# Perceiver block on one core: loop order of the cross-attention, keys and values between the scores and the turns of the probabilities

## The reference, cut to what matters

```
q = (layernorm(x) @ wq.T + bq)          # 16 heads of 8
k = (ctx @ wk.T + bk);  v = (ctx @ wv.T + bv)
scores = einsum('bhqd,bhkd->bhqk', q, k) / sqrt(8)
attn = softmax(scores, axis=-1)          # over 257 keys
x = x + einsum('bhqk,bhkd->bhqd', attn, v) @ wo.T + bo
x = x + neighbour_mix(layernorm(x))
x = x + experts(layernorm(x))            # top 2 of 8, F = 512
```

## Time and profile before

| | |
|---|---|
| runs | 288.32, 285.59, 285.55 us |
| profiled execution | 286.31 us, span 284.6 us |
| PE busy | 217.0 us, 76% of the span |
| DVE busy | 157.0 us, 55% |
| ACT busy | 137.6 us, 48% |
| POOL busy | 133.8 us, 47% |
| mean granted clock of PE | 0.937 |
| attention loop, first maxima of batch 0 to the last `take_output` | 17.8 to 137.9 us |

### The profile page before, as it was taken

One profiled execution on the slowest core, in us unless ns is written; L12 is line 12 of the kernel. 1 busy time (PEld: TensorE's weight loads), 2 busy tenths in 40 slices (PEclk: granted clock), 3 DMA queues, 4 the chain that ended last, 5 costly groups with the idle time before them and its releaser, 6 DMA issues.

```text
span 284.6 us, 6292 instructions
## 1 busy us (share of the span) xinstructions
PE 217.0 (76%) x2039; PEld 171.1 (60%) x2039; DVE 157.0 (55%) x515; ACT 137.6 (48%) x419; POOL 133.8 (47%) x243
## 2 busy tenths in 40 slices
PE   0859999999999999998669831599877677859520
PEld 0636666766666666665437431499867667749510
DVE  3346677777777777877463785155433433323310
ACT  2437777777777777788034320345333143233100
POOL 2635454545454545242433406636656566645442
PEclk9998999999999999999999975599999999997965
DMA  7752223131405000000000252212222222223100
GB/s 222 260 212 77 113 57 130 40 149 13 176 10 176 2 2 2 2 0 2 3 0 0 75 121 31 51 17 29 31 36 23 28 37 29 30 31 26 9 2 0
DMA packets 12432, 16.06 MB, mean 56 GB/s; under 512 B 2561, under 2 KB 8834, under 8 KB 12402
## 3 DMA queue, kind: packets, MB, share of 16 engines
q1 hardware_dynamic: 8354, 13.08, 14.5%
q0 software_dynamic: 4048, 2.59, 7.5%
HBM read 13.02 MB, written 3.10 MB: 57 GB/s over the span
## 4 chain that ended last, share of the span: by engine, by line
PE 51%; DMA 25%; DVE 10%; issue 6%; POOL 3%; SPq 1%; POOLq 1%; ACT 0%; DVEq 0%; ACTq 0%
DMA out<-y_sb,y_tok 22%; PE bank L649 12%; PE bank L622 8%; PE bank L639 8%; PE bank L671 7%; PE bank L624 5%; PE bank L784 4%; DMA ctx_sb<-ctx_keys 2%; DVE y_sb L1058 2%; PE bank L656 1%; DMA slot_sb<-table,slot_row 1%; PE bank L794 1%; DVE stats L835 1%; POOL row_in_tile L446 1%; PE bank L716 1%
## 5 line engine op out<-in xcount | busy, mean ns | idle before, releaser
L515 ACT ACTIVATE p_sb<-bank,neg_max 128x257 f32<-128x257 f32 x128 | 59.1, 474 | 8.5 <-DVE neg_max L881 8.5
L881 DVE TENSOR_REDUCE neg_max<-bank 128x1 f32<-128x257 f32 x128 | 45.5, 418 | 30.0 <-PE bank L639 30.0
L464 POOL DMA_INDIRECT out<-y_sb,y_tok x23 | 36.4, 1581 | 38.0 <-DVE slot_meta L1039 24.4
L784 PE MATMUL bank<-slot_ft,w_now 128*128 128x128 f32 x368 | 49.3, 282 | 0.7 <-ACT slot_ft L565 0.4
L784 PEld LDWEIGHTS bank<-slot_ft,w_now 128*128 128x128 f32 x368 | 46.6, 199 | 1.1 <-ACT slot_ft L565 0.7
L794 PE MATMUL bank<-wo_sb,hid_ft 128*128 x184 | 27.1, 293 | 20.1 <-DVE y_sb L1058 20.1
L649 PE MATMUL bank<-ident,p_sb 128*128 128x128 f32 x256 | 36.7, 287 | 0.9 <-ACT p_sb L515 0.9
L794 PEld LDWEIGHTS bank<-wo_sb,hid_ft 128*128 128x128 f32 x184 | 23.4, 199 | 23.1 <-issue 23.1
L649 PEld LDWEIGHTS bank<-ident,p_sb 128*128 128x128 f32 x256 | 27.4, 143 | 13.6 <-issue 10.7
L565 ACT ACTIVATE slot_ft<-bank 128x128 f32<-128x128 f32 x23 | 6.4, 278 | 55.0 <-PE bank L773 51.1
L377 POOL COPY sum_last<-p_sb 128x4 f32<-128x4 f32 x32 | 6.1, 191 | 50.9 <-ACT p_sb L515 50.9
(11 more groups left out here) (146 smaller groups left out, 333.4 us busy)
## 6 DMA issues: line engine op xcount, KB each, us to landing
ctx_sb<-ctx_keys SPq DMA_DIRECT2D x8, 512.0 KB, 4.3
w_sb<-w SPq DMA_DIRECT2D x8, 512.0 KB, 4.8
wo_sb<-wo SPq DMA_DIRECT2D x8, 256.0 KB, 5.6
table<-rows_tok SPq DMA_DIRECT2D x2, 520.0 KB
x_tok<-x SPq DMA_DIRECT2D x2, 256.0 KB, 3.2
out<-x_tok SPq DMA_DIRECT2D x1, 512.0 KB, 3.2
w_sb<-weights SPq DMA_DIRECT2D x1, 384.0 KB, 4.3
slot_sb<-table,slot_row POOLq DMA_INDIRECT x23
```

What stands on the lines that cost most here:

```text
L464: pool.indirect_dma_start(out, bass.IndirectOffsetOnAxis(y_tok[s % 2][:], 0), y_sb[s % 2][:], None, bounds_check=last_token, oob_is_err=Fa ...
L515: act.activation(p_sb[b % 2][:, g, :], s_bank[g][:, 0:SKV], ACT.Exp, bias=neg_max[b % 2][:, g:g + 1], accum_out=sum_last[:, 0, b, g:g + 1] ...
L784: last = pe.matmul(bank[2 * m + s % 2][:, tile(c)], w01_now[s % 2][:, m, tile(c)], slot_ft[s % 2][:], start=True, stop=True)
L881: dve.tensor_reduce(neg_max[b % 2][:, g:g + 1], s_bank[g][:, 0:SKV], AX.X, ALU.max, negate=True).then_inc(max_ready, 1)
```

## The change

Only the order of steps in the loops is changed; no instruction is added or taken away, and none changes its size or what it waits for. On PE, `keys_values` moves from the end of a round to behind the next round's `scores`, and it is the batch two ahead there. On ACT, `keys(b+1)` and `turned(b-1)` stand behind `softmax(b)`. On DVE `take_output` moves from the head of a round to the end of the round before. On POOL `add_heads` runs one round earlier.

```diff
 # POOL
-            for b in range(B + 3):
+            for b in range(B + 2):
                 if b + 2 < B:
                     last_key(b + 2)
                 if b % BPT == 0 and b + BPT < B:
                     queries(b // BPT + 1)
                 if 1 <= b <= B:
                     keep_last(b - 1)
-                if b >= 3:
-                    add_heads(b - 3)
+                if b >= 2:
+                    add_heads(b - 2)
                 if b % BPT == 1 and b > BPT:
                     spread_scales(b // BPT - 1)
 # ACT
             keys(0)
-            for b in range(B + 2):
+            for b in range(B + 1):
+                if b < B:
+                    softmax(b)
                 if b + 1 < B:
                     keys(b + 1)
-                if b >= 2:
-                    turned(b - 2)
-                if b < B:
-                    softmax(b)
+                if b >= 1:
+                    turned(b - 1)
 # PE
+            scores(0)
             keys_values(1)
-            scores(0)
-            keys_values(2)
             for b in range(B):
                 if b + 1 < B:
                     scores(b + 1)
+                if b + 2 < B:
+                    keys_values(b + 2)
                 turn_probs(b)
                 if b >= 1:
                     weigh_values(b - 1)
-                if b + 3 < B:
-                    keys_values(b + 3)
             weigh_values(B - 1)
 # DVE
             values(0)
-            for b in range(B + 3):
-                if b >= 3:
-                    take_output(b - 3)
-                    if b - 3 >= BPT and (b - 3) % BPT == 0:
-                        finish_tile((b - 3) // BPT - 1)
+            for b in range(B + 2):
                 if b < B:
                     maxima(b)
                 if b + 1 < B:
                     values(b + 1)
                 if 1 <= b <= B:
                     turned(b - 1)
                 if b >= BPT and b % BPT == 0:
                     scale_tile(b // BPT - 1)
+                if b >= 2:
+                    take_output(b - 2)
+                    if b - 2 >= BPT and (b - 2) % BPT == 0:
+                        finish_tile((b - 2) // BPT - 1)
```

## The result

The changed kernel took 304.64 us (median of 4 runs, 303.60 to 306.51) against 285.57: 1.066 times the time before, with a 95% interval of 1.059 to 1.073. The forecast was 304.3, range 301.3 to 309.0.

A forecast was written before the change was run, and what follows sets the result against it. Before, a ring from PE over DVE (3.63 us a batch) was the bound; after, one over ACT and DVE (4.02). Start -1.57, loop +19.1, end +1.18 give +18.7: 305.0 profiled, median 304.3, range 301.3 to 309.0.

The forecast's parts named there:

- The ring: In the batch loop, ACT's key copy and DVE's value copy stand in series: 4.02 us a batch, from 3.63.
- The handover: From ACT's key copy to DVE's value copy, taken as 0.06 us, with bounds of 0.02 and 0.20.
- The tile steps: On DVE between turned copy and next maxima: `scale_tile` adds 0.41 us and `finish_tile` 0.78 a tile.
- Spread: In the loop, PE waits about 0.6 us for POOL's `spread_scales`, covered by `finish_tile`; uncovered, 0.3 us a tile would show.
- Start: Up to the first maxima of batch 1: they come at 20.87 us against 22.44, 1.57 won.
- End: After the loop, the last tile's `spread_scales` stands behind `add_heads(31)` and comes 1.18 us later.
- The clock: Rival: PE's idle time in the loop lowers its clock, PE becomes the bound, +41 us, about 326; chance 4%.
- The second wait: Rival: POOL or PE 0.5 us late around `spread`, seven tiles pay 0.3 to 0.7 each, 306 to 309; chance 12%.
- The other sign: Rival: the ring over ACT stays under 3.63 us, PE alone bounds the loop, 278.7 us; chance 3%.
- PE's move alone: On PE, L622 and L624 behind the scores would alone give PE back its idle 0.21 us a batch.

The follow-up runs named there:

- the turned wait: The change, with DVE's value copy waiting for PE alone and ACT's key copy waiting for that value copy: 286.99 us, 1.003 of before.
- the dose: The change, with ACT's key copy behind three exponentials (291.83 us) or behind two (284.69 us), where the change has it behind all four.
- the spread put first: The change, with `spread_scales` ahead of `add_heads` in POOL's round: 302.65 us, 1.061 of before.

## Why the prediction was right, step by step

- **The ring**: 4.00 measured, 4.02 reckoned, from 3.63 before. Shown by the turned wait (17.7 us back with no list changed) and by the dose (0.455 per exponential). The handover that no row of before showed is 0.03 (the key copy ends at 74.44, the value copy starts at 74.47); I had taken 0.06 out of 0.02 to 0.20. DVE idled 45.0 us before the value copy and not 48: 1.45 a batch and not 1.55, since the four maxima fill DVE for 1.41 and I had taken 1.34, the time to the start of the next instruction.
- **The tile steps**: rounds of 4.37 and 4.78 (twice 4.88), reckoned 4.43 and 4.80. From the first maxima of batch 1 to those of batch 31 it took 149.06 - 20.42 = 128.6 us, reckoned 128.7. That it is so near is in part luck, for small errors cancel. Too much were 0.06 a scaled tile and 0.02 a plain round, together 0.7. Too little was the first round, 4.21 for 3.82, in which PE worked at the low clock; twice a finish, by 0.1; and once a round of 4.59, where `side_constants` on POOL held a softmax by 0.2.
- **Spread**: PE waited 0.59 for it (reckoned 0.6), and `finish_tile` covered it as said. Its removal changed no pitch.
- **Start**: 22.44 - 20.42 = 2.0 won, reckoned 1.57. The step that was off is the clock: I had the scores of batch 1 at the low level, but they ran in 0.71 and the clock fell just behind them (the next L622 took 0.98, the turns of batch 0 1.91 where later ones took 1.04).
- **End**: +1.0, reckoned 1.18, and shown by the spread put first.
- **The rest**: nothing was reckoned, and in the profiled executions it is +2.2: from the last `scale_rows` to the end 149.2 us against 147.0. The eight further kernels, with the same work there, took 146.3 to 148.0. I count it as scatter of the expert stage; part of it may be a granted clock of 0.91 in a stretch where before had 1.00. What sets that is open. -2.0 + 19.0 + 1.0 + 2.2 is the 20.2 between the profiled executions; the medians lie 19.1 apart. The three terms that were reckoned measured 18.0 together, for 18.7. So part of the nearness of 304.3 to 304.64 is luck: the terms were 0.7 too large, and about 1 us came from a stage for which nothing was reckoned.
- **The rivals.** The clock fell once at the start of the loop, for most of a stretch (mean 0.59 from 20.3 to 24.5 us), as it did in the kernel before (0.64 from 19.6 to 24.3). From 24.5 to 149 us it stayed at 1.00, with PE busy 13.60 of 17.24 us, 79%. So the gaps that the ring opens, each near 1 us, were no ground for a fall here. The Trainium skill (TensorE: Matmul & The Clock Gate, "Part 1: The HAM clock gate") says that the clock is halved after idle time; that gaps as short as these are enough, as the prediction read it, it doesn't say, and this trace speaks against it. The second wait did not come. The other sign did not come either. Its point was that the ring stays under 3.63 if the key copy ends 2.44 us or less behind the first maximum. That holds for plain rounds alone: with the copy behind three exponentials it ended at 2.37 and they took 3.55, but the steps of the tiles (3.91 and 4.49) kept the kernel at 291.8. With the copy behind two (about 1.9) it became level with before.
- **The range.** Its upper end was taken too low: the prediction's own terms give 304.3 + 4 + 0.5 + 1.4 = 310.2 and not 308. The measured time does not turn on it.

One statement of the prediction was wrong, though no term of the sum rests on it: that PE's move alone would give PE back its 0.21 us a batch. With PE's new order and ACT's old one the kernel took 318 us, the slowest of all that ran (POOL's order, changed there too, was worth 1.0 us). So the fault is not ACT's order alone. The place that works lies between: behind PE's keys of the same round, ahead of the last two exponentials.

## What to carry to other kernels

When loops with offsets are turned, write for each copy which round it belongs to before and after, and not only what kind of instruction it follows: here DVE's list and the kinds in ACT's list were the same, and one copy a batch later made a ring. Then add up each closed way through two engines from starts to starts; the longest is the pitch, and work that sat in an idle engine before (the tile's steps) counts nearly in full once its engine is in the ring (here 0.37 and 0.78 a tile). A copy that several engines wait for belongs where its producer has just finished, in the midst of a long step if need be: earlier in the list, its own engine waits for the producer (1.86 us a batch here), later, the others wait for the copy. And steps without a hurry belong where an engine waits anyway.

## What the runs showed of the hardware

A handover from ACT to DVE took 0.03 us (key copy to value copy, in the change), one from DVE to ACT 0.12 (the first of four maxima is about 0.41 long, and the exponential starts 0.53 behind its start). In the change the granted clock fell behind a pause of PE of 1.73 us at the start of the loop, and stayed at 1.00 from 24.5 to 149 us, through pauses before the scores of about 1 us in most batches (1.2 at most). The expert stage and what leads to it varied by 2.9 us (146.3 to 149.2) between ten kernels with the same instructions there, with the clock granted in it differing; a change under 1% needs the stretch that it touches, besides the whole time.
